# Two VectorE steps of a four-layer residual kernel, moved from among the shared expert tiles to between the first batch's two expert tiles

## The reference, cut to what matters

```
x = x + (x @ W_base.T + b_base + 2 * sum_e cond[b, e] * (x @ As[e].T @ Bs[e].T))      # layer 0
x = x + (x @ (sum_g cond[b, g] * weight[g] * mask).T + bias)                          # layer 1
# layer 2: two experts of eight for each batch, and one shared expert for all
p = softmax(cond); w, sel = top_k(p, 2); w = w / sum(w)
x = x + sum_k w[b, k] * mlp(x, skill[sel[b, k]]) + mlp(x, shared)    # mlp: (gelu(x @ gate) * (x @ up)) @ down
# layer 3: the one expert with the largest cond
e = argmax(cond[b]); up = x @ W_up[e].T + b_up[e]; gate = x @ W_gate[e].T + b_gate[e]
x = x + (silu(up) * gate) @ W_down[e].T + b_down[e]
```

## Time and profile before

| what | value |
|---|---|
| median of 3 runs | 92.47 us (92.28 to 92.53) |
| profiled execution, its own time | 92.08 us |
| its span, first to last instruction | 90.3 us |
| TensorE busy | 83.2 us, 92% of the span |
| VectorE busy | 54.5 us, 60% |
| ScalarE busy | 28.0 us, 31% |
| GpSimd busy | 16.3 us, 18% |
| TensorE's granted clock | 1.000 of full speed |

### The profile page before, as it was taken

How to read it: one execution, slowest core, us unless ns; L and a number is a source line. 1 busy time by engine, 2 the same in 40 slices (tenths; PEclk the granted TensorE clock), 3 DMA queues, 4 the chain that set the end, 5 groups by cost and what they waited for, 6 DMA issues and landing times.

```text
span 90.3 us, 1922 instructions
## 1 busy us (share of the span) xinstructions
PE 83.2 (92%) x620; PEld 77.3 (86%) x620; DVE 54.5 (60%) x123; ACT 28.0 (31%) x49; POOL 16.3 (18%) x19
## 2 busy tenths in 40 slices
PE   5999775999999799999999999999999999999950
PEld 5948673888887698999999999999999999999730
DVE  0249999899999533245465465465456547445770
ACT  2305580383727552202402402402302312211120
POOL 3246450046555970000000000000000000000000
PEclk9999999999999999999999999999999999999999
DMA  2994000769992000188489889988998888625001
GB/s 43 362 388 191 0 0 0 261 199 354 425 399 115 0 0 0 22 313 301 125 321 337 259 288 335 283 261 283 307 324 348 285 289 301 226 37 183 2 29 33
DMA packets 5768, 18.57 MB, mean 206 GB/s; under 512 B 640, under 2 KB 1920, under 8 KB 5760
## 3 DMA queue, kind: packets, MB, share of 16 engines
q1 hardware_dynamic: 5472, 18.16, 58.0%
q10 hardware_dynamic: 288, 0.32, 1.2%
HBM read 17.95 MB, written 0.52 MB: 205 GB/s over the span
## 4 chain that ended last, share of the span: by engine, by line
PE 63%; DVE 23%; DMA 5%; issue 4%; ACT 1%; ACTq 0%; DVEq 0%
PE bank L626 32%; PE bank L636 16%; PE bank L650 7%; DMA rest_sb<-in_rest 5%; DVE hid L442 5%; PE bank L666 4%; DVE p L345 2%; DVE wsel L423 1%; DVE p L353 1%; DVE val L362 1%; PE bank L597 1%; DVE eq L372 1%; DVE eq L361 1%; DVE hot L405 1%; PE bank L598 1%
## 5 line engine op out<-in xcount | busy, mean ns | idle before, releaser
L626 PE MATMUL bank<-x_t,pair_w 128*128 128x128 f32 (+1 forms) x256 | 31.3, 275 | 0.5 <-DVE hid L442 0.5
L626 PEld LDWEIGHTS bank<-x_t,pair_w 128*128 128x128 f32 x256 | 29.9, 192 | 0.8 <-issue 0.8
L444 DVE SCALAR_TENSOR_TENSOR hid<-gelu,wsel,bank 128x512 f32<-128x512 f32 x16 | 12.0, 748 | 21.8 <-PE bank L626 19.0
L279 ACT ACTIVATE gelu<-bank 128x512 f32<-128x512 f32 x24 | 14.1, 593 | 31.6 <-PE bank L626 27.6
L636 PE MATMUL bank<-hid,pair_w 128*128 128x128 f32 x128 | 16.9, 275 | 0.0
L636 PEld LDWEIGHTS bank<-hid,pair_w 128*128 128x128 f32 x128 | 15.7, 192 | 0.1
L247 POOL TENSOR_TENSOR hid_l<-hid,hid_h 128x512 fp32r<-128x512 f32 x8 | 10.2, 1286 | 10.1 <-ACT hid_h L298 10.1
L650 PE MATMUL bank<-x_t,w 128*128 128x128 f32 x64 | 8.7, 276 | 0.0
L650 PEld LDWEIGHTS bank<-x_t,w 128*128 128x128 f32 x64 | 7.9, 192 | 0.1
L285 ACT ACTIVATE tanh<-half 128x256 f32<-128x256 f32 (+1 forms) x9 | 3.5, 392 | 13.4 <-DVE half L473 13.4
L597 PE MATMUL bank<-x_h,shared_h 128*128 128x512 f32 x16 | 6.4, 399 | 1.1 <-DVE x_h L391 1.1
(11 more groups left out here) (67 smaller groups left out, 76.6 us busy)
## 6 DMA issues: line engine op xcount, KB each, us to landing
pair_w<-in_skill SPq DMA_DIRECT2D x16, 768.0 KB, 5.7
w<-in_layer SPq DMA_DIRECT2D x8, 384.0 KB, 5.4
shared_sb<-in_shared SPq DMA_DIRECT2D x3, 256.0 KB, 5.3
w_sb<-in_w SPq DMA_DIRECT2D x1, 576.0 KB, 4.5
x_t<-in_x SPq DMA_DIRECT2D x2, 256.0 KB, 4.0
out_x<-out_sb SPq DMA_DIRECT2D x8, 64.0 KB, 4.2
rest_sb<-in_rest ACTq DMA_DIRECT2D x1, 181.0 KB, 4.7
head_sb<-in_head ACTq DMA_DIRECT2D x1, 132.0 KB, 3.2
```

Of the source, the lines that this page charges most:

```text
L279: act.activation(gelu[:, n, :], ps[:, :], ACT.Gelu_apprx_tanh).then_inc(gelu_ready, 1)
L444: dve.scalar_tensor_tensor(hid[:, n, :], gelu[:, n, :], wsel[:, bass.DynSlice(weight, 1)], u_ps[n][:, :], ALU.mult, ALU.mult).then_inc(hid ...
L626: mm = pe.matmul(ps[:, S * t:S * (t + 1)], pair_w[:, slot, n, 128 * t:128 * (t + 1)], x2_t[:, columns(b)], start=True, stop=True)
```

## The change

Only VectorE's stream is edited. After `hidden(4)`, `bias_columns()` no longer follows, and after `hidden(5)`, `add_shared(0)` no longer follows. Both now stand between `hidden(8)` and `hidden(9)`, the two expert tiles of batch 0, `add_shared(0)` first. The call of `batch(0, 0, last=False, before_last=False)`, which issued just these two `hidden` steps, is written out as two calls. No instruction is added or removed.

```diff
-            between = {0: lambda: stream2_rest(1), 1: softmax, 2: chosen_probabilities, 3: expert_weights, 4: bias_columns,
-                       5: lambda: add_shared(0)}
+            between = {0: lambda: stream2_rest(1), 1: softmax, 2: chosen_probabilities, 3: expert_weights}
             for k in range(NSH):
                 hidden(k, k % 2)
                 if k in between:
                     between[k]()
-            batch(0, 0, last=False, before_last=False)
+            hidden(NSH, 0, 0)
+            add_shared(0)
+            bias_columns()
+            hidden(NSH + 1, 1, 1)
             add_shared(1)
             batch(1, 1, before_last=False)
```

## The result

The changed kernel is slower. Its median is 93.30 us over 22 runs, that of the kernel before 92.69 us over 22 runs. One of the 22 runs of the changed kernel took 472.41 us; it is left out of the ratio, which is of the fast runs alone. The ratio is 1.0052, with a 95% interval of 1.0031 to 1.0073. I had forecast 92.41 us and no measurable difference. Later runs of the same two kernels gave 1.0060 (1.0029 to 1.0091) and 1.0031 (1.0000 to 1.0062).

The account below looks back on a forecast made before the run. TensorE was taken to set the end, standing still only in a 0.73 us wait before gate_up(0, 0). Only that wait was to change, by -0.06 us: 92.47 - 0.06 = 92.41 us, range 92.12 to 92.60.

Parts of the forecast that it names:

- the hole: TensorE's wait between shared tile 4's last down matmul and gate_up(0, 0): 0.73 us, all there is to win.
- Part 1: Ahead of hidden(6), 1.73 us leaves VectorE's stream; hidden(5) moves from 28.13 to 27.01 us, hidden(4) stays.
- Part 2: hidden(6) still waits for tile 4's hid_l on GpSimd, ending at 29.14 us; gain 0.06 us (0.00 to 0.18).
- The issue entry of 0.11 us: Chain entry before hidden(6), 29.23 to 29.34 us, read as fitting its release after hid_l's end.
- Rival 2: At hidden(6): nothing moves, as release and issue already set its start at 29.34; 92.47 us, chance 0.20.
- Part 3: Between hidden(8) and hidden(9): the moved steps delay hidden(9) by up to 0.56 us, free within 2.35 us slack.
- rival 3: At down(0, 1): TensorE waits for a late hidden(9), making the kernel slower, 93.0 us; chance 0.03.
- Rival 1: At the joint before gate_up(0, 0): VectorE's queue alone holds hidden(6), the whole wait closes, -0.73 us, 91.74; chance 0.06.
- The level: Whole kernel: the median before the change, taken as 92.47 us, from which the forecast gain was subtracted.
- The chances: Whole kernel: faster 0.10, same 0.86, slower 0.04, with differences over 0.3% counted as measurable.

Follow-up runs that it names:

- e2: The changed kernel with four needless waits early in VectorE's stream, compiled to two more instructions; ratio to the kernel before 1.0013.
- e3: The changed kernel with add_shared(0) back in its old place, so only bias_columns is moved; ratio to the kernel before 1.0016.
- e4: The changed kernel with bias_columns back in its old place, so only add_shared(0) is moved; ratio to the kernel before 0.9974.
- e6: The kernel before, old order, with 256 needless waits (128 instructions) early in VectorE's stream; ratio to the kernel before 1.0939.
- e7: The changed kernel with two needless waits early in VectorE's stream, compiled to one more instruction; one run, 92.70 us.
- e8: The changed kernel with expert_weights moved too, from after hidden(3) to after hidden(7); ratio to the kernel before 0.9883.
- e9: The kernel before with only expert_weights moved, from after hidden(3) to after hidden(7); ratio to the kernel before 0.9912.
- e5: The kernel before, old order, with 248 needless waits (124 instructions) early in VectorE's stream; ratio to the kernel before 1.0983.
- e8_repeat: The same kernel as e8, run once more for its time; ratio to the kernel before 0.9915.

## Why the prediction was wrong, point by point

- **What bounds the kernel, and the hole.** Right. TensorE is busy without a break on both sides of it, and what the hole gains or loses is what the span gains or loses.
- **Part 1, what leaves the stream.** Right: `hidden(5)` starts 0.60 us behind `hidden(4)`.
- **Part 2, what is late next.** The wait for hid_l is the right one: in e2, e3, e4, e6 and e7 `hidden(6)` starts 0.07 to 0.08 us behind the matmul that the same hid_l releases, and H is 0.91. That is 0.06 below the kernel before, the gain that I had given; my 0.14 us from hid_l's end to `hidden(6)`, that is D 0.09 and H 0.91, was right. The step that failed is the sentence behind it, "how soon after 29.14". I bounded the start by 0.05 and 0.14 us after hid_l's end and by no change at all, so neither end held a loss. The runs put 0.43 us more there. My reasoning was on work and waits; a move also shifts each instruction's number, and that had a price of its own. The row of 0.47 us of issue at 27.57 stood in the trace of before, under `bias_columns`, that is, under the cover which the change took away.
- **The issue entry of 0.11 us** I took for the release by hid_l. It was VectorE's own pace: `hidden(6)` starts 0.61 us behind `add_shared(0)` before, 0.60 in e6, as `hidden(5)` behind `hidden(4)` in the changed kernel. VectorE's queue and hid_l end within 0.07 us of each other in the old order, so moving the two steps could win no more than that. Rival 2 took the same 0.11 us for a bound, and falls too: without the stall `hidden(6)` does move.
- **Part 3, and rival 3.** No loss at `hidden(9)`: it starts at 36.24, its reader is at 39.92, and `bias_hot` took 0.48 us, behind the last hid_l. Rival 3 had the sign of the result and not its cause. Its price was real, though: `bias_hot` started 0.26 us after that hid_l had ended (34.65 and 34.91), and e9 shows 1.25 us for it where the two meet.
- **Rival 1** fell as argued; e8 and e9 show that the whole 0.73 us is to be had, but by an earlier `hidden(4)`.
- **The level.** I took 92.47 us from three runs. The 22 runs of the kernel before give 92.69, so its own median already lies above my range of 92.12 to 92.60, and "nothing moves" would have missed the range as well. Of the 0.89 us between 92.41 and 93.30, 0.22 are this level and 0.43 the stall; the other 0.24 no view places. By the ratio the loss is 0.48 us, of which H explains 0.37, and the rest is within the interval.
- **The chances.** 0.04 for slower was far too low. All cases were drawn from waits, and none from the instruction stream.

The Trainium skill, Runtime: NRT & Kernel Launch, section "Instruction fetch mechanics", says that instructions come in blocks by the sequencer's own transfers and that crossing a boundary is mostly hidden. The runs agree as far as the kernel before goes (0.06 us). They disagree where the crossing falls on an instruction that is released late: 0.43 us in full. The page's block is 16 KiB; here the packets that go with VectorE's places are of 8 KiB, and a shift by 128 instructions brings the stall back.

What is shown: the position in the stream makes and removes the stall, at one instruction, at 64 and at 192, in three orders of work (the changed kernel, e5, e9), with an instruction packet 0.66 to 0.68 us behind. That the sequencer spends the 0.4 us on passing from one block to the next is the plain reading, but no run shows it.

## What to carry to other kernels

Before an engine's steps are moved, read the "issue" entries of its chain that lie under other work. One of 0.4 us that is covered now is a debt, and an edit that shifts the stream or uncovers it can call it in; a needless instruction or two, put where the engine waits anyway, moves it away. And ask which input of a late step was last: here it was the result of a step two tiles back, so shortening the queue right ahead of it was worth 0.06 us, and shortening the queue ahead of that earlier step 0.74 us.

## What the runs showed of the hardware

- The stall that comes with an instruction packet for VectorE costs 0.35 us (e5 against e6) to 0.43 us (the changed kernel against e2) at one instruction, seen at two places 128 instructions apart. It costs nothing to 0.06 us if that one is under other work or is a wait with time to spare.
- In e8 `wpart`, 16 elements wide with one input, took 1.21 us beside a hid_l on GpSimd, against 0.17 in the earlier trace rows, and ended 0.04 us behind that hid_l (32.60 and 32.56); e8_repeat has 1.20. I had taken one input for safe; it is not in this form (a tensor times one constant). `wnorm`, a multiplication with two inputs just before it, took 0.76. `wpart` is number 64 there, but its packet came at 31.09, before it started, so the fetch doesn't explain its length.
- `bias_hot`, with two inputs, took 1.25 us beside hid_l in e9, against 0.48 in the kernel before.
